# Attention on one core: five heads' factors on GpSimd in place of four, with the steps around them moved

## The reference, cut to what matters

```
q, k, v  = heads of x @ Wq.T + bq, x @ Wk.T + bk, x @ Wv.T + bv        # x here is the layer norm of x
scores   = q . k / 16**0.5                                             # (b, h, i, j)
li, lj   = x @ rel_W[:, :d].T, x @ rel_W[:, d:].T                      # three relations
probs    = softmax over the 3 relations of (li[i] + lj[j] + rel_b)     # (b, i, j, 3)
bias     = probs @ logical_bias.T                                      # (b, h, i, j)
gate     = sigmoid(x @ gate_W.T + gate_b)                              # one value per token and head
out      = softmax_j(scores + gate * bias) @ v @ Wo.T + bo
x        = x + out
```

## Time and profile before

| | before |
|---|---|
| median of 3 runs | 6042.36 us (6042.21 to 6044.77) |
| profiled execution, its own time | 6042.3 us |
| span of the profiled execution | 6040.5 us |
| busy shares of the span | PE 89%, DVE 78%, ACT 73%, POOL 61% |
| one attention tile that carries all side work | 43.28 us |
| one attention tile of the last batch | 42.10 us |

### The profile page before, as it was taken

One profiled execution on the slowest core, in us unless ns is written; L12 is line 12 of the kernel. 1 busy time (PEld: TensorE's weight loads), 2 busy tenths in 40 slices (PEclk: granted clock), 3 DMA queues, 4 the chain that ended last, 5 costly groups with the idle time before them and its releaser, 6 DMA issues. The chain is left out here.

```text
span 6040.5 us, 114022 instructions
## 1 busy us (share of the span) xinstructions
PE 5365.8 (89%) x40162; PEld 3532.6 (58%) x40162; DVE 4701.5 (78%) x6099; ACT 4409.7 (73%) x7005; POOL 3704.9 (61%) x2010
## 2 busy tenths in 40 slices
PE   6888888898989898888799869999999979999999
PEld 4666666666666666655344345555555546666665
DVE  6999999999999999998888679999999942122221
ACT  4999999999999999999366678888888821111111
POOL 3888888888888888875100079999999930000000
PEclk8999999999999999999899889999999989999999
DMA  2121121212112121200355555555555521111110
GB/s 74 28 49 31 28 51 28 51 28 51 28 34 45 30 48 31 46 17 14 129 190 211 187 211 187 208 208 191 195 201 207 184 101 42 45 35 35 35 35 11
DMA packets 461255, 537.80 MB, mean 89 GB/s; under 512 B 237537, under 2 KB 337761, under 8 KB 460785
## 3 DMA queue, kind: packets, MB, share of 16 engines
q1 hardware_dynamic: 460784, 531.75, 28.0%
HBM read 370.31 MB, written 161.35 MB: 88 GB/s over the span
## 5 line engine op out<-in xcount | busy, mean ns | idle before, releaser
L502 DVE CUSTOM_DVE_ANT_0 srow<-srow,ps_s,small 128x1024 f32<-128x1024 f32 x1024 | 1304.0, 1273 | 63.5 <-issue 34.6
L576 ACT ACTIVATE srow<-srow,nmax 128x1024 f32<-128x1024 f32 x1024 | 1200.0, 1172 | 87.3 <-DVE nmax L502 78.3
L585 ACT COPY AT<-ps_t 128x512 f32<-128x512 f32 x2048 | 1110.5, 604 | 19.8 <-PE ps_t L658 18.8
L658 PEld LDWEIGHTS ps_t<-ident,srow 128*128 128x128 f32 x8192 | 954.9, 141 | 224.2 <-issue 36.3
L658 PE MATMUL ps_t<-ident,srow 128*128 128x128 f32 x8192 | 1068.7, 273 | 2.8 <-ACT AT L585 2.4
L1977 POOL TENSOR_TENSOR c_hc<-c_hs,c_cs 128x1024 f32<-128x1024 f32 x432 | 1009.9, 2364 | 61.2 <-DVE c_hs L2079 59.1
L491 DVE SCALAR_TENSOR_TENSOR srow<-ps_p,rho,R 128x1024 f32<-128x1024 f32 x768 | 975.3, 1270 | 0.0
L1938 PE MATMUL c_ps_y<-c_hc,c_ident 128*128 128x512 f32 x2048 | 944.8, 594 | 29.9 <-DVE c_y L2062 21.4
L2079 DVE TENSOR_TENSOR_SCAN c_hs<-c_da,c_pd 128x1024 f32<-128x1024 f32 x384 | 860.1, 2273 | 54.6 <-PE c_pd L1929 54.6
L647 PE MATMUL ps_s<-K,Q 96*128 96x512 bf16 x2048 | 617.1, 383 | 291.2 <-DVE nmax L502 265.3
L2022 ACT ACTIVATE c_sT<-c_dxT,c_bT 128x256 f32<-128x256 f32 x1536 | 668.4, 494 | 107.0 <-PE c_pd L1929 96.9
(11 more groups left out here) (256 smaller groups left out, 8576.5 us busy)
## 6 DMA issues: line engine op xcount, KB each, us to landing
c_cs<-bc_d SPq DMA_DIRECT2D x256, 512.0 KB, 4.3
c_bs<-bc_d SPq DMA_DIRECT2D x64, 512.0 KB, 6.5
Q<-parts_d SPq DMA_DIRECT2D x384, 64.0 KB, 2.3
parts_d<-parts SPq DMA_DIRECT2D x57, 384.0 KB, 3.4
K<-parts_d SPq DMA_DIRECT2D x168, 128.0 KB, 4.4
sz_d<-b_sz SPq DMA_DIRECT2D x16, 1024.0 KB, 7.1
xv_d<-b_xv SPq DMA_DIRECT2D x16, 1024.0 KB, 7.8
dt_d<-b_ab SPq DMA_DIRECT2D x16, 1024.0 KB, 4.2
```

The costliest lines, as they stand in the source:

```text
L502: nc.vector.tensor_tensor_reduce(r[:], r[:], ps_s[:], small[:, slot, h:h + 1], BIG, ALU.add, ALU.min, nmax[:, h % NROW:h % NROW + 1]).then ...
L576: nc.scalar.activation(r[:], r[:], ACT.Exp, scale=-1.0, bias=nmax[:, h % NROW:h % NROW + 1]).then_inc(e_ok, 1)
L585: nc.scalar.copy(AT[h % NAT][:, HG * half:HG * half + HG, :], ps_t[:, half]).then_inc(at_ok, 1)
L658: last = nc.tensor.transpose(ps_t[:, half, i, :], rows_sb[h % NROW][:, j * P:(j + 1) * P], ident[:])
```

## The change

The list `POOL_HEADS` gets five heads, (1, 4, 7, 10, 13), in place of (1, 4, 8, 12). GpSimd's program becomes: f(4), rem, rel twice, rstd, lo, f(7), sum twice, f(10), t, f(13), ge, xrb, p twice, gT, f(1) of the next tile, kappa. On VectorE `dve_v` moves from slot 4 to slot 5 and now follows `dve_xn`, `dve_y` moves from slot 10 to slot 11, and `dve_xn` becomes a `scalar_tensor_tensor` whose second tensor is `rstd` broadcast over the columns, in place of a `tensor_scalar`. On ScalarE `act_o` moves from slot 5, ahead of that slot's transposed copies, to the end of slot 4, and the exponential of `act_y0` moves from behind e(8) to ahead of it.

```diff
-    POOL_HEADS = (1, 4, 8, 12)
+    POOL_HEADS = (1, 4, 7, 10, 13)
...
         def dve_xn(dve, p, k):
             wait(dve, rstd_ok, p + 1)
-            nc.vector.tensor_scalar(xn[:], xt[:, k, :], mv[:, 0:1], rstd[:, 0:1],
-                                    ALU.subtract, ALU.mult).then_inc(x_free, 1)
+            nc.vector.scalar_tensor_tensor(xn[:], xt[:, k, :], mv[:, 0:1], rstd[:, 0:1].broadcast_to([P, D]),
+                                           ALU.subtract, ALU.mult).then_inc(x_free, 1)
...
-                pool_f(pool, t, k, 8)
+                pool_f(pool, t, k, 7)
                 for n in range(2 * look):
                     pool_sum(pool, t + 1, 1 - k, n)
-                pool_f(pool, t, k, 12)
+                pool_f(pool, t, k, 10)
+                if look:
+                    pool_t(pool, t + 1)
+                pool_f(pool, t, k, 13)
+                if pro:
+                    pool_ge(pool, t + NT)
                 if post:
                     pool_xrb(pool, t - 1)
-                if look:
-                    pool_t(pool, t + 1)
-                if pro:
-                    pool_ge(pool, t + NT)
                 for n in range(2 * look):
                     pool_p(pool, t + 1, 1 - k, n)
...
                     if pro and u == 5:
                         dve_xn(dve, t + AHEAD, 1 - k)
-                    if pro and u == 4:
+                    if pro and u == 5:
                         dve_v(dve, t + NT, 1 - par, ib)
                     if post and u == 6:
                         dve_norm(dve, t - 1)
-                    if look and u == 10:
+                    if look and u == 11:
                         dve_y(dve, t + 1)
...
                 for u in range(H):
+                    if look and u == 8:
+                        act_y0(act, t + 1, 1)
                     act_e(act, t, u)
-                    if post and u == 5:
-                        act_o(act, t - 1)
                     if pro and u == 7:
                         act_xT(act, t + AHEAD)
-                    if look and u in (7, 8):
-                        act_y0(act, t + 1, u - 7)
+                    if look and u == 7:
+                        act_y0(act, t + 1, 0)
...
                     if look and u in (1, 3, 4):
                         act_rel(act, t + 1, 1 - k, after(par, ib, 1), (1, 3, 4).index(u))
+                    if post and u == 4:
+                        act_o(act, t - 1)
```

## The result

The changed kernel takes 6054.89 us (median of 17 runs; 16 took 6048.73 to 6062.3, and one of 12088.73 is left out of the ratio) against 6042.29 (6038.47 to 6046.08) for the kernel before. The ratio is 1.002, with a 95% interval of 1.0013 to 1.0028: +12.6 us, slower by 0.2%, against a forecast of 6051. The profiled execution took 6057.01 us, its span 6055.2.

The account below looks back on a forecast made before the run. The prediction took a loop through ScalarE, GpSimd and VectorE, not one engine, to bound the kernel. Full tiles +3 and the last batch +6 made +9 on 6042.3: 6051, likeliest case 6038 to 6062, 8 in 10 6018 to 6074.

Parts of the forecast that it names:

- The full tile: Attention tiles with layer-norm work: 43.33 us against 43.27, +0.06 a tile over 55 tiles, +3 us.
- The path through s(7): VectorE's way to the y0 exponential, starting it at 24.80; the later of two, against 24.65 along ScalarE.
- rival A: GpSimd's chain is not last; TensorE and VectorE pace tiles at 42.6 to 42.8: 6012 to 6003; chance 0.20 with partial form.
- The port: VectorE and GpSimd exclude each other at the shared SBUF port, the later instruction waiting, at 1.08 us a meeting.
- The last batch: Tiles without gT and qk: L474 waits for f(4)'s L410, +1.25 for six tiles, about 1 given back, +6 us.
- f(4)'s L408 0.6 before s(0): Last batch: f(4)'s L408 starts 0.6 before s(0), so L474 meets L410 and s(1) starts at 4.75, not 3.55.
- The moves costed at nothing: o to slot 4, v's later slot, xrb and ge behind f(13), kappa and rem: no cost beyond the sum.
- B: Same GpSimd chain a little longer, y serial between f(13) and p: tiles 43.55 to 43.6, 6066; chance 0.25.
- C: In full tiles L474 meets f(4)'s L410 and waits about 2 us: +1.6 a tile, some 6135; chance 0.08.
- D: The change doesn't bring five factors to GpSimd; excluded by the list, as L410's count must rise by 64.

Follow-up runs that it names:

- 2: Changed kernel with xn as `tensor_scalar` again: 6049.52 us, ratio 1.0014 to the kernel before.
- experiment 3: Changed kernel with xn in slot 4, ahead of f(7)'s L410: 6055.84 us, ratio 1.0023 to the kernel before.
- after: The changed kernel itself, with all parts of the change made to the kernel before: 6054.89 us.
- 1: Changed kernel with only the y0 exponential put back behind e(8): 6118.35 us, ratio 1.0125 to the kernel before.
- experiment 8: Kernel before, with only the y0 exponential moved ahead of e(8): 6007.54 us, ratio 0.9946.
- experiment 7: Changed kernel with f(13) ahead of t on GpSimd: 6061.71 us, ratio 1.0026 to the kernel before.
- 5: Changed kernel without head 13 on GpSimd, VectorE making f(13) itself: 6105.12 us, ratio 1.0104 to the kernel before.
- 6: Changed kernel with xrb moved from behind f(13) to behind f(1): 6100.09 us, ratio 1.0095 to the kernel before.
- experiment 4: Changed kernel with L474 moved from slot 0 to slot 1 in the last batch: 6048.19 us, ratio 1.001 to the kernel before.
- 9: Changed kernel with `act_o` back in slot 5, behind e(5): 6099.36 us, ratio 1.0095 to the kernel before.
- 12: Changed kernel with f(13) ahead of t, xrb behind f(1), and the last batch's rel steps both in slot 1: 6035.55 us, ratio 0.9987.
- experiment 10: Kernel before, with the y0 exponential ahead of e(8), v in slot 5 and o in slot 4: 6091.11 us, ratio 1.0077.

## Why the prediction was right, and where its sizes were off

**The full tile** went by the steps given, at times within 0.1 of them, counted from s(0) at 1396.96:

| step | predicted | measured |
|---|---|---|
| y0 exponential starts | 24.80 | 24.71 |
| t starts | 26.05 | 25.97 |
| f(13)'s L410 ends | 32.08 | 32.03 |
| xrb done, p starts | 33.98 | 33.90 |
| gT ends | 39.74 | 39.67 |
| s(15) | 40.64 | 40.56 |
| next s(0) | 43.33 | 43.25 |

The path through s(7) was given as the later of two to the exponential. s(7) comes at 20.19, where 20.2 to 20.3 was said, and the exponential 0.09 sooner than said; all behind it kept that. With s(7) made earlier (experiments 2 and 3) a tile gains only 0.07, so the other path, ScalarE's own, lies close behind. The term was +0.06 a tile, +3 us, where a usual tile measured -0.03, 43.24 against 43.27, -2 us in all. From the start of the attention to the L474 at 2522.55 the changed kernel is 3.3 ahead; the rest of that lies in odd tiles (two of 45.6 and 46.4 us before, one of 45.9 after), which the change isn't shown to cause.

The mechanism (the 1.04 that ScalarE gives is eaten by f(13) and by y, one after the other on the port) is shown by experiments 1 and 8: undo the exponential's move and +1.03 a tile appears; make it without the fifth factor and the other moves, and 35 us are gained; in experiment 7, where y finds the port free, the quick tiles take 42.64.

Two of the working's readings were loose. It has VectorE work through from y to s(0), where its own rows show waits of 0.37 and 0.22, and of the 1.04 only 0.55 reached the tile in experiment 8. And by its own terms the lower end of rival A is 6001, not 6003.

**The port.** L440 at 1.68, L482 at 1.88 and L447 waiting for gT came as stated. GpSimd's busy time of a full tile was given as 40.1 and measured 41.21: its own waits for the port, 0.96 in `ge` above all, were not counted. The Trainium skill's rule in "SBUF — State Buffer", section "Who interferes with whom", of an exclusive lock, held in after and in experiments 1, 5, 6 and 7: the later one ended after the earlier one each time, as L482 did 1.07 after L410.

**The last batch was mis-sized:** +6 predicted, about +14 measured (from 3.3 ahead at 2522.55 to 10.5 behind at the last L516, 2880.0 against 2869.5). The first tile is 0.1 quicker than before, the next five are 1.6 to 3.7 slower and the stretch behind the last L474 is 2.7 slower, where +1.25 a tile was given and 1 us was to come back at the ends. GpSimd's timeline, VectorE's and TensorE's, after:

```profile
2607.11 1.11 POOL L408 TENSOR_SCALAR srow<-R,rho 128x1024 f32<-128x1024 f32 x1
2608.40 2.37 POOL L410 TENSOR_TENSOR srow<-srow,R 128x1024 f32<-128x1024 f32 x1 [0.18 <-POOL srow L408]
```

```profile
2607.39 1.28 DVE L502 CUSTOM_DVE_ANT_0 srow<-srow,ps_s,small 128x1024 f32<-128x1024 f32 x1 [0.22 <-DVE srow L491]
...
2608.60 2.72 DVE L474 TENSOR_SCALAR RT<-Dj,small 128x1024 f32<-128x1024 f32 x1
...
2612.43 1.26 DVE L502 CUSTOM_DVE_ANT_0 srow<-srow,ps_s,small 128x1024 f32<-128x1024 f32 x1
```

```profile
2613.76 0.61 PE L647 MATMUL ps_s<-K,Q 96*128 96x512 bf16 x2 [2.53 <-DVE nmax L502]
2614.20 1.13 PE L658 MATMUL ps_t<-ident,srow 128*128 128x128 f32 x8
2615.13 1.92 PE L694 MATMUL ps_m<-w_o,O 128*128 128x256 f32 x4
```

The step that was given as "f(4)'s L408 0.6 before s(0)" measured 0.28, so L474 met the L410 sooner in its run and waited longer: s(1) came at 5.04, not 4.75. Meanwhile TensorE sat idle for 2.53, and then its granted clock fell; windows of 1 us show it:

```profile
2613.00:2614.00 1.00, 0.24 (x2) 0.12 (x3) 1.00 (x3) 0.26 (x1) 0.00 (x0) 1.00 0.00 0
...
2615.00:2616.00 1.00, 1.00 (x6) 0.82 (x5) 1.00 (x1) 1.00 (x3) 0.92 (x1) 0.51 0.00 0
2616.00:2617.00 1.00, 1.00 (x3) 0.32 (x1) 1.00 (x2) 0.91 (x1) 1.00 (x1) 0.50 0.00 0
```

0.50 is the level of 1.2 GHz. L694, 1.03 before, takes 1.92. No step of the sum had that. What the clock costs here can be read from experiment 3, whose tiles of the last batch have the same program. In two of them the clock stays:

```profile
2606.91:2650.58 43.67, 34.19 (x426) 24.14 (x426) 39.70 (x50) 39.85 (x57) 35.55 (x19) 1.00 0.09 21
```

The waits alone thus make 43.67 of 42.10, +1.6 where +1.25 was given. The fallen clock adds 0.3 to 0.5, and 2.1 in the tile of 45.82, where it lasts longer. Experiment 4 takes L474's wait away and gets 41.85 where the clock stays and 43.4 where it falls. Why it falls in one tile and not in the next is open.

Of the remaining 4 us between the two profiled executions (spans 14.7 apart, 10.5 at the end of the attention) the rows show only that they lie in later parts, which the change doesn't touch; the medians are 12.6 apart.

**The total** came within 4 us of the forecast partly by luck. The full tiles and the odd ones came 6 us lower than the sum had them and the last batch 8 higher, and the later parts, at nothing in the sum, gave 4 in the profiled pair.

**The moves costed at nothing.** For xn and its form it is shown within 0.07 a tile, 3 to 4 us (3, 2). For o it is true of the move as made, but the cover was thinner than the text let one think: 44 us without it (9). The 0.7 us of xrb and the fifth factor itself both delay gT; with xrb moved, or the factor given back to VectorE, the kernel is slower all the same (6, 5).

**The rivals.** A, the gain, doesn't come in after, but 7 and 12 show its tile (42.6 to 42.8). B's figure, 6066, was too high by 11: the chain was shorter by 0.08, not longer. C is real, though in no usual full tile of after: L474 takes 2.94 in after's second tile (46.75 long, 46.71 before) and about 2.7 in the last batch, it is a part of the loss in 5, and it parts the two kinds of tile in 7. It is the nearest danger to any edit of this order. D: L410 rose to 320.

## What to carry to other kernels

An engine pair that shares a port has an order of its own, beside the queues: list which instruction starts first at each meeting, because 0.1 us there decided over 0.8 to 2 us (6, 7), and an edit that frees the other engine can move a meeting to the wrong side. When a change is a bundle, run its parts alone: here one moved exponential was worth -35 us and the rest of the bundle +47 (6054.9 less 6007.5). And price a wait by what the waiting engine's neighbours do afterwards, TensorE's granted clock included.

## What the runs showed of the hardware that was not expected

- After short idle times TensorE's granted clock fell to 0.50 for some 3 us: 2.53 us idle in the last batch of after (and once for nearly 7 us, behind 2.55 idle), 2.00 in experiment 4, 1.55 in experiment 10, where a tile then took 1.52 us longer. In other tiles the same 2.53 (experiment 3), the same 2.00 and the same 1.55 left it at 1.00. What tells them apart was not settled.
- One program had two kinds of tile for long stretches of the same execution, 42.6 and 44.6 (experiment 7), told apart by which of L474 and L410 got the port first. Their starts lie within 0.3 us of each other; where L410 was down as starting 0.04 behind L474, it went either way (L474 0.75 in one tile, 2.96 in another).
- The port works in both directions: y waited 0.8 for L410, and the 128x16 `ge` behind it took 1.24 instead of 0.28.
- What was left after a wait was nearly the whole instruction: L482 ended 1.07 after the end of the L410 that it had waited for, only 0.15 less than its whole length of 1.22. Its overlap with L410 was 0.81; it cost VectorE 0.66, and GpSimd 0.96 more at `ge`.
